# A two-layer graph network on one core: layer norm 2's sums on ScalarE, small factors on GpSimd, T1's four sums on VectorE, and new orders on every engine

## The chip, the cores and the metric

One core of one Trainium2 chip runs the whole program in one launch. The metric is the device time of one execution in microseconds (us), median of several runs. The core's engines are TensorE (PE in the profile, PEld for its weight loads), VectorE (DVE), ScalarE (ACT), GpSimd (POOL) and SyncE (SP), which here issues all the DMAs.

## The reference, cut to what matters

There are 128 graphs, each with 128 nodes and 512 features. For each graph (fp32):

```python
h  = relu(layernorm(x))                              # layer norm 0
A  = adj + I;  D = A.sum(-1) ** -0.5
x1 = x + (A * D[:,None] * D[None,:]) @ (h @ W + b)   # layer 0
xh = relu(layernorm(x1))                             # layer norm 1
H  = (adj != 0);  w = adj[0]                         # edge weights: the first row
P  = H @ diag(1/H.sum(0)) @ H.T;  dn = 1/(H @ w), 0 where H @ w is not positive
z  = relu(dn * (P @ (xh @ W1.T)) + b1)               # 1024 wide
hn = layernorm(z) * gamma + beta                     # layer norm 2
out = x1 + xh + dn * (P @ (hn @ W2.T)) + b2
```

## The kernel before, in words

The unit of work is a pair of graphs, `p` (64 pairs, `NP`); `g` is a graph (128, `NG`), `k` the number of a step of the steady loop. Every fp32 matrix is split into two fp16 parts, high and low, and every product is three matmuls (high by high, high by low, low by high). The high part is made by ScalarE, the low part by VectorE, so both stand in the chain of each product.

TensorE does for each graph `Y0` (h by W, 12 matmuls of 512 columns into the bank `ps_e`), `Z0` (A by that, 3, into the same bank `ps_e`), `T1` (xh by P, 12 short ones into `ps_t`), `U` (hn by W2, 24, into `ps_u`) and `Y2` (P by that, 3, into `ps_y2`). For each pair the product by W1 is one step of a Strassen-like scheme: seven products `M1` to `M7` of 6 matmuls each into `ps_x`, `ps_y`, `ps_z`, instead of eight. `P(p)` makes the matrix P and, in a 129th column, H @ w for both graphs in `ps_p`.

VectorE takes `Y0` out of `ps_e` (`yv`, then `yl`), and `x1(g)` takes `Z0` out of `ps_e` and adds x. `Y0` of the next graph waits for that `x1`, since both use `ps_e`. `z1` to `z7` take the seven products out of PSUM and add them into `zh`. `do_h` (ScalarE) is the relu on `zh`; `do_s2` and `do_aggr2` (VectorE) take mean and variance of 1024 values by batch-norm statistics; `do_u2`, `do_sc2` (GpSimd) and `do_nm2` (VectorE) turn them into scale and bias; `do_hn` (ScalarE) applies them; `do_hn_hi` (ScalarE) and `do_hn_lo` (VectorE) split the result, which DMAs transpose for `U`. After `U`, `do_uh` (ScalarE) and `do_ul` (VectorE) split it for `Y2`, and `do_out` (VectorE) makes the result.

The scheme of seven products needs four sums of quarters of T1 (`S1` to `S4`, 128x256 fp32), which GpSimd makes in SBUF once both `T1` are kept (`do_tf`); `do_thS` and `do_tlS` split them. GpSimd also makes `x1b`, `scr2` and `base2` (the part x1 + xh + b2 of the result, 128x512 fp32) and the small factors `rd0`, `cx`, `u1`, `sc1`, `dn1`, `dn2`, `qdn`.

The order on each engine is a list written out by hand. It has a beginning, a loop over pairs (`for k in range(STEADY_FROM, STEADY_TO)`) in which each engine works on several pairs at different stages, and an end. Engines meet by semaphores: `done(eng, s, n)` waits until `s` has counted to `n`, and `landed` waits for a DMA. In the names that the profile prints, buffer numbers are left out and aliases show as the tensor they lie in: `raw_w` is `zh`, `y`, `yh`, `yl`, `uh`, `ul`, `vq` or the result, `bet_wide` is `hn_hi` or `hn_lo`, `raw_t` is the transposed hn, `b_all` is `x1b` or `b1_all`, and `ps_y` is `ps_y` or `ps_y2`.

Of the kernel before, what the change touches and what calls it, by code (L numbers as in the profile page):

```python
# [5 lines left out]
def bass_adjacency_prenorm_two_layer_gnn_kernel(  # L6
# [52 lines left out]
    with ctx:  # L59
# [173 lines left out]
        def _(sp):  # L233
# [95 lines left out]
            do_ldX(10); do_tr0h(8); do_tr0h(9); do_trl(0); do_tr0l(8); do_trh(1); do_tr0l(9); do_ldA(10); do_trl(1)
            do_trA(6); do_ldX(11); do_ldX(12); do_trh(2); do_trl(2); do_tr0h(10); do_ldA(11); do_st(0); do_tr0l(10)  # L330
            do_tr0h(11); do_st(1); do_trh(3); do_tr0l(11); do_trl(3); do_ldX(13); do_trA(7); do_ldw(9); do_trh(4)
            do_ldA(12); do_trl(4); do_ldw(10); do_tr0h(12); do_st(2); do_tr0l(12); do_trh(5); do_st(3); do_ldX(14)
            do_tr0h(13); do_tr0l(13); do_trl(5); do_trA(8); do_ldX(15); do_trh(6); do_ldA(13); do_trl(6)
            do_tr0h(14); do_ldw(11); do_st(4); do_tr0l(14); do_trh(7); do_st(5); do_ldX(16); do_trl(7); do_tr0h(15)
            do_tr0l(15); do_trA(9); do_ldX(17); do_ldA(14); do_tr0h(16); do_trh(8); do_trl(8); do_ldw(12); do_st(6)
            do_tr0l(16); do_trh(9); do_st(7); do_trl(9); do_ldX(18); do_tr0h(17); do_tr0l(17); do_ldw(13)
            do_trA(10); do_ldX(19); do_ldA(15); do_trh(10); do_trl(10); do_tr0h(18); do_tr0l(18); do_st(8)
            do_trh(11); do_st(9); do_trl(11); do_ldX(20); do_tr0h(19); do_tr0l(19); do_ldw(14); do_trA(11)
# [1201 lines left out]
```

## Time and profile before

| | us |
|---|---|
| median of 3 runs | 1993.31 (1990.59 to 1993.95) |
| the profiled execution, its own time | 1991.01 |
| its span, first to last instruction | 1989.2 |
| TensorE busy | 1884.0 (95%) |
| VectorE busy | 1845.1 (93%) |
| ScalarE busy | 1292.1 (65%) |
| GpSimd busy | 1039.0 (52%) |

The span leaves 1.8 us of the execution's own time outside it. A busy share is a mean over the beginning, the loop and the end, which have different limits. The granted clock of TensorE has a mean of 0.99 of full speed over the span.

### The profile page before, as it was taken

The numbers are of one execution on the slowest core, as the hardware profiler recorded it, in microseconds if no ns is written. First come the engines' busy times: TensorE is split into PE (matmuls) and PEld (weight loads), VectorE is DVE, ScalarE is ACT, GpSimd is POOL, SyncE is SP. The second block draws the span as 40 slices with busy tenths as digits, with TensorE's granted clock in tenths as the row PEclk, the third lists the DMA queues.
The fourth block names the chain that finished last, engine by engine and source line by source line (L and its number), as shares of the span: only waits on it lengthen the run. The fifth ranks groups of instructions, "written<-read, shape, count | busy, mean of one in ns | idle before, by whom it ended". The sixth has DMA issues, their size and how long they took to land. (4 is left out here: it accounts for less than half of the span.)

```text
span 1989.2 us, 36929 instructions
## 1 busy us (share of the span) xinstructions
PE 1884.0 (95%) x9926; PEld 898.9 (45%) x9926; DVE 1845.1 (93%) x3751; ACT 1292.1 (65%) x2342; POOL 1039.0 (52%) x1234
## 2 busy tenths in 40 slices
PE   4688999999999999999999999999999999999998
PEld 2334444444444444444444444444444444444443
DVE  7999999999999999999999999999999999998864
ACT  5766666766766666676676676676667667667553
POOL 3656555455555555555546545555555554654541
PEclk9889999999999999999999999999999999999999
DMA  8235354544445445445444544544544444444333
GB/s 210 46 74 108 81 107 105 93 102 108 97 95 108 98 97 108 102 101 104 105 91 104 107 96 100 108 101 96 107 102 99 104 102 94 102 100 86 83 64 75
DMA packets 536734, 197.57 MB, mean 99 GB/s; under 512 B 484944, under 2 KB 501328, under 8 KB 536528
## 3 DMA queue, kind: packets, MB, share of 16 engines
q1 hardware_dynamic: 536528, 195.21, 46.9%
q8 instruction: 82, 1.34, 0.3%
q14 instruction: 124, 1.02, 0.2%
HBM read 48.31 MB, written 33.55 MB: 41 GB/s over the span
## 5 line engine op out<-in xcount | busy, mean ns | idle before, releaser
L381 PE MATMUL ps_u<-w2h,raw_t 128*128 128x512 f16 x2048 | 484.7, 379 | 6.7 <-DVE raw_w L1051 6.1
L1392 POOL TENSOR_TENSOR base<-b_all,xh 128x512 f32<-128x512 f32 x128 | 210.1, 1641 | 352.7 <-DVE raw_w L1060 344.4
L381 PEld LDWEIGHTS ps_u<-w2h,raw_t 128*128 128x128 f16 x2048 | 198.6, 98 | 252.4 <-issue 22.9
L381 PE MATMUL ps_u<-w2l,raw_t 128*128 128x512 f16 x1024 | 241.9, 379 | 0.0
L1046 DVE TENSOR_TENSOR bet_wide<-raw_w,bet_wide 128x1024 f16<-128x1024 f32 x128 | 211.3, 1650 | 8.4 <-ACT bet_wide L714 8.1
L681 ACT ACTIVATE tS<-ps_t 128x512 f32<-128x512 f32 x128 | 76.2, 595 | 205.2 <-PE ps_t L371 205.0
L638 ACT ACTIVATE raw_w<-v_all,qdn 128x512 f32<-128x512 f32 x128 | 85.8, 714 | 164.9 <-POOL qdn L1437 162.8
L1397 POOL TENSOR_TENSOR base<-base,raw_w 128x512 f32<-128x512 f32 x128 | 182.4, 1425 | 19.3 <-ACT raw_w L638 1.7
L1359 POOL TENSOR_TENSOR rd<-u,neg_half 128x4 f32<-128x4 f32 x64 | 70.0, 1094 | 201.8 <-DVE u L900 201.7
L381 PE MATMUL ps_e<-w0h,h0T_hi 128*128 128x512 f16 x512 | 134.6, 386 | 34.2 <-DVE x L939 34.0
L1386 POOL TENSOR_TENSOR b_all<-x,b_all 128x512 f32<-128x512 f32 x128 | 164.8, 1287 | 1.3
L1026 DVE BATCH_NORM_STATS2 raw<-raw_w 128x6 f32<-128x512 f32 x256 | 160.6, 671 | 2.5 <-ACT raw_w L700 2.5
L705 ACT ACTIVATE raw_w<-raw_w,nm,sc 128x1024 f32<-128x1024 f32 x128 | 156.7, 1232 | 7.1 <-DVE nm L1038 5.9
L392 PE MATMUL ps_x<-w1h,th 128*128 128x512 f16 x512 | 152.9, 380 | 5.2 <-issue 4.8
L381 PEld LDWEIGHTS ps_u<-w2l,raw_t 128*128 128x128 f16 x1024 | 100.2, 98 | 120.8
L392 PE MATMUL ps_x<-w1l,th 128*128 128x512 f16 x512 | 152.7, 380 | 0.0
L392 PE MATMUL ps_x<-w1h,tl 128*128 128x512 f16 x512 | 152.7, 380 | 0.0
L983 DVE SCALAR_TENSOR_TENSOR raw_w<-ps_x,dn,b_all 128x512 f32<-128x512 f32 x192 | 142.4, 742 | 3.9 <-PE ps_x L392 3.9
L700 ACT ACTIVATE raw_w<-raw_w 128x1024 f32<-128x1024 f32 x128 | 134.7, 1053 | 8.8 <-DVE raw_w L983 8.4
L714 ACT ACTIVATE bet_wide<-raw_w 128x1024 f16<-128x1024 f32 x128 | 134.0, 1047 | 6.5 <-DMA raw_t<-bet_wide 6.5
L381 PE MATMUL ps_e<-w0l,h0T_hi 128*128 128x512 f16 x512 | 134.0, 385 | 0.0
L381 PE MATMUL ps_e<-w0h,h0T_lo 128*128 128x512 f16 x512 | 132.3, 381 | 0.0
(151 smaller groups left out, 4517.5 us busy)
## 6 DMA issues: line engine op xcount, KB each, us to landing
x_t<-in_x_dram SPq DMA_DIRECT2D x128, 256.0 KB, 2.9
out_dram<-raw_w SPq DMA_DIRECT2D x128, 256.0 KB, 2.4
adj_t<-in_adj_dram SPq DMA_DIRECT2D x64, 128.0 KB, 2.1
raw_t<-bet_wide SPq DMA_TRANSPOSE x256, 3.2
w_col<-in_adj_dram SPq DMA_DIRECT2D x128, 0.5 KB, 2.2
raw_w<-in_W1T_dram SPq DMA_DIRECT2D x4, 512.0 KB, 4.8
h0T_hi<-h_hi SPq DMA_TRANSPOSE x128, 2.5
h0T_lo<-h_lo SPq DMA_TRANSPOSE x128, 2.4
```

Source lines behind the costliest of these rows:

```text
L381: mm = pe.matmul(ps, t[:, j * 128:(j + 1) * 128], w[:, j, :], start=(n == 0 and j == 0), stop=(n == 2 and j == blocks - 1))
L392: mm = pe.matmul(ps[:, :], t[:, t_at - 1, j * 128:(j + 1) * 128], w[:, w_at, j, :], start=(begins and n == 0 and j == 0), stop=(n == 2 and ...
L638: act.activation(vq[:, j, :], v_all[:, :], ACT.Copy, scale=qdn[:, p % 2, j:j + 1]).then_inc(s_vq, 1)
L700: act.activation(zh[:, g % 4, :], zh[:, g % 4, :], ACT.Relu).then_inc(s_h, 1)
L705: act.activation(zh[:, g % 4, :], zh[:, g % 4, :], ACT.Identity, bias=nm2[:, p % 2, j:j + 1], scale=sc2[:, p % 2, j:j + 1]).then_inc(s_hn, 1)
L714: act.activation(hn_hi[:, :], zh[:, g % 4, :], ACT.Copy).then_inc(s_hnh, 1)
L983: return dve.scalar_tensor_tensor(out=z, in0=bank[:, :], scalar=dn1[:, p % 2, j:j + 1], in1=z if row is None else row[:, cols], op0=ALU.mu ...
L1026: dve.bn_stats(raw2[:, g % 2, c, :], zh[:, g % 4, c * CH:(c + 1) * CH]).then_inc(s_rw2, 1)
L1046: dve.tensor_tensor(hn_lo[:, :], zh[:, g % 4, :], hn_hi[:, :], ALU.subtract).then_inc(s_hnl, 1)
L1386: pool.tensor_tensor(x1b[:, :], x1[:, g % 4, :], b2_all[:, :], ALU.add).then_inc(s_x1b, 1)
L1392: pool.tensor_tensor(base[:, g % 6, :], x1b[:, :], xh[:, g % 2, :], ALU.add).then_inc(s_scr2, 1)
L1397: pool.tensor_tensor(base[:, g % 6, :], base[:, g % 6, :], vq[:, g % 2, :], ALU.add).then_inc(s_base2, 1)
```

## The change

Five things change, and then all orders.

1. Layer norm 2. `do_h` also sums its output while it applies the relu (`hsum`). VectorE makes minus the mean of both graphs of the pair in one small operation (`do_nmu`). ScalarE squares `zh` with that as bias and sums it (`do_sq`, once for each graph, its product thrown away into `sq_scrap`), and GpSimd makes scale and bias. `do_s2`, `do_aggr2` and VectorE's `do_nm2` are gone.
2. `do_bias0`, `do_nm1` and `do_nm2` go to GpSimd; the first two are done for one graph at a time (128x1), and ScalarE waits for its own graph's.
3. The four sums `do_S1` to `do_S4` go from GpSimd to VectorE, with the same operation and size.
4. `do_dn` reads H @ w from PSUM (`ps_pp[:, :, N]`) and no longer from `dm` in SBUF, and the next `P` waits for it and no longer for `do_dm`.
5. The orders: the loop runs from pair 5 and no longer from pair 7, and to `NP - 16` and no longer `NP - 9`, and the order in the loop, in the beginning and at the end is another on every engine. SP's list loads `adj` of the first pairs ahead of its edge weights. No matmul and no DMA is added or taken away.

```diff
-    STEADY_FROM, STEADY_TO = 7, NP - 9
+    STEADY_FROM, STEADY_TO = 5, NP - 16
-            do_ldw(0); do_ldA(0); do_ldw(1); do_ldA(1); do_ldw(2); do_ldA(2); do_ldw(3); do_ldX(0); do_ldX(1)
+            do_ldA(0); do_ldw(0); do_ldA(1); do_ldw(1); do_ldA(2); do_ldw(2); do_ldX(0); do_ldX(1); do_ldA(3)
...
-                done(pe, s_dm, p)
+                done(pe, s_dn, p)
...
-                act.activation(zh[:, g % 4, :], zh[:, g % 4, :], ACT.Relu).then_inc(s_h, 1)
+                done(act, s_nmu, p - 1)
+                act.activation(zh[:, g % 4, :], zh[:, g % 4, :], ACT.Relu, accum_out=hsum[:, p % 2, j:j + 1]).then_inc(s_h, 1)
+
+            def do_sq(g):
+                p, j = g // 2, g % 2
+                act.wait_ge(s_nmu, p + 1)
+                done(act, s_u2, p - 1)
...
+                done(act, s_sq, g)
+                act.activation(sq_scrap, zh[:, g % 4, :], ACT.Square, bias=nmu[:, p % 2, j:j + 1],
+                               accum_out=ssq[:, p % 2, j:j + 1]).then_inc(s_sq, 1)
...
                 dve.wait_ge(s_ri, p + 1)
+                dve.wait_ge(s_p, p + 1)
...
-                dve.scalar_tensor_tensor(out=dn[:, p % 2, :], in0=dm[:, :], scalar=TINY, in1=ri[:, :],
+                dve.scalar_tensor_tensor(out=dn[:, p % 2, :], in0=ps_pp[:, :, N], scalar=TINY, in1=ri[:, :],
                                          op0=ALU.is_gt, op1=ALU.mult).then_inc(s_dn, 1)
 
+            def do_nmu(p):
+                dve.wait_ge(s_h, 2 * p + 2)
+                done(dve, s_sq, 2 * p - 2)
+                done(dve, s_ln2, p - 1)
+                dve.tensor_scalar(nmu[:, p % 2, :], hsum[:, p % 2, :], -1.0 / DH, None, ALU.mult).then_inc(s_nmu, 1)
...
             def do_u2(p):
-                pool.wait_ge(s_stat2, 2 * p + 2)
+                pool.wait_ge(s_sq, 2 * p + 2)
...
+            def do_nm1(g):
+                p, j = g // 2, g % 2
+                pool.wait_ge(s_pp1, p + 1)
+                done(pool, s_xh, g - 3)
+                pool.tensor_scalar(nm1[:, p % 2, j:j + 1], st1[:, p % 2, j, 0:1], sc1[:, p % 2, j:j + 1], -1.0,
+                                   ALU.mult, ALU.mult).then_inc(s_ln1, 1)
```

How the loop's orders move is seen at three places. On TensorE, in the loop before, this is the piece from `Z0` of the even graph (`ps_e`, line 432) over `M5` and `T1` to `Y0` of the odd graph (`ps_e`, line 381); twelve rows of `T1` stand in it:

```order
L432 MATMUL ps_e<-raw_w,A_HT 128x512
L433 MATMUL ps_e<-raw_w,A_HT 128x512
L434 MATMUL ps_e<-raw_w,A_HT 128x512
L392 MATMUL ps_z<-w1h,th 128x512 x2
L392 MATMUL ps_z<-w1l,th 128x512 x2
L392 MATMUL ps_z<-w1h,tl 128x512 x2
L369 MATMUL ps_t<-P_hi,xh_hi 128x128
L370 MATMUL ps_t<-P_lo,xh_hi 128x128
L371 MATMUL ps_t<-P_hi,xh_lo 128x128
```

In the loop of the change `Z0` (line 444 now) is followed by `Y2` of an older graph (`ps_y`), the twelve rows of `T1` and `M7` (`ps_x`), and then comes `Y0` (line 393):

```order
L444 MATMUL ps_e<-raw_w,A_HT 128x512
L445 MATMUL ps_e<-raw_w,A_HT 128x512
L446 MATMUL ps_e<-raw_w,A_HT 128x512
L444 MATMUL ps_y<-raw_w,P_hi 128x512
L445 MATMUL ps_y<-raw_w,P_hi 128x512
L446 MATMUL ps_y<-raw_w,P_lo 128x512
L381 MATMUL ps_t<-P_hi,xh_hi 128x128
L382 MATMUL ps_t<-P_lo,xh_hi 128x128
L383 MATMUL ps_t<-P_hi,xh_lo 128x128
```

So the three matmuls of a `Y2` more lie between the even graph's `Z0` and the odd graph's `Y0` (nine matmuls of 512 columns and a `T1`, six and a `T1` before).

On VectorE, around the same `x1` (`x<-ps_e,cx,x_t`, line 939), the loop before has, behind a `z2` (`ps_y`), a result (`base`), `hn_lo` of the odd graph (`bet_wide`) and `P_lo`:

```order
L983 SCALAR_TENSOR_TENSOR raw_w<-ps_y,dn,raw_w 128x512
L1060 SCALAR_TENSOR_TENSOR raw_w<-ps_y,dn,base 128x512
L1046 TENSOR_TENSOR bet_wide<-raw_w,bet_wide 128x1024
L1125 TENSOR_TENSOR P_lo<-ps_p,P_hi 128x256
L939 SCALAR_TENSOR_TENSOR x<-ps_e,cx,x_t 128x512
L1130 TENSOR_SCALAR dm<-ps_p 128x2
```

and in the change the same `x1` (line 1002 now) stands behind a result, `h0_lo` and `z6` (`ps_x`), ahead of the second result and `P_lo`:

```order
L1097 SCALAR_TENSOR_TENSOR raw_w<-ps_y,dn,base 128x512
L978 TENSOR_TENSOR h_lo<-h,h_hi 128x512
L1039 SCALAR_TENSOR_TENSOR raw_w<-ps_x,dn,b_all 128x512
L1002 SCALAR_TENSOR_TENSOR x<-ps_e,cx,x_t 128x512
L1097 SCALAR_TENSOR_TENSOR raw_w<-ps_y,dn,base 128x512
L1167 TENSOR_SCALAR dm<-ps_p 128x2
L1162 TENSOR_TENSOR P_lo<-ps_p,P_hi 128x256
```

`hn_lo` of the odd graph is gone from in front of this `x1`; it stands at the end of the step now, ahead of the four sums.

On GpSimd, the loop before has from the four sums (`tS`) to `rd0` the factors of layer norm 2 (`u<-st`, `sc`), and then those of layer norm 1 (`u<-st,eps_t`, `sc`):

```order
L1407 TENSOR_TENSOR tS<-tS 128x256
L1402 TENSOR_TENSOR tS<-tS 128x256
L1411 TENSOR_TENSOR tS<-tS 128x256
L1415 TENSOR_TENSOR tS<-tS 128x256
L1442 TENSOR_SCALAR u<-st 128x2
L1447 TENSOR_TENSOR sc<-u,neg_half 128x2
L1373 TENSOR_TENSOR u<-st,eps_t 128x2
L1378 TENSOR_TENSOR sc<-u,neg_half 128x2
L1359 TENSOR_TENSOR rd<-u,neg_half 128x4
```

and in the change `u1` and `sc1` of layer norm 1 come first, then `u2` (`u<-ssq`, which waits for both sums of squares), and behind it the two `nm1` (`nm<-st,sc`) for which ScalarE's `xh` waits:

```order
L1482 TENSOR_TENSOR u<-st,eps_t 128x2
L1487 TENSOR_TENSOR sc<-u,neg_half 128x2
L1533 TENSOR_SCALAR u<-ssq 128x2
L1553 TENSOR_SCALAR nm<-st,sc 128x1 x2
L1539 TENSOR_TENSOR sc<-u,neg_half 128x2
L1559 TENSOR_TENSOR nm<-nmu,sc 128x2
L1468 TENSOR_TENSOR rd<-u,neg_half 128x4
L1546 TENSOR_SCALAR bias<-st,rd 128x1 x2
```

The four sums are gone from GpSimd, and the two `nm1` of layer norm 1 are queued behind layer norm 2's `u2`. ScalarE's loop ends with the second `do_sq`, and the next step begins with `do_uh`, one `do_cntH` and the two `do_xh`.

## Rows read from the trace of the kernel before

**Rows 1.** The page: the span and each engine's busy time, share and instructions.

```profile
span 1989.2 us, 36929 instructions
PE 1884.0 (95%) x9926; PEld 898.9 (45%) x9926; DVE 1845.1 (93%) x3751; ACT 1292.1 (65%) x2342; POOL 1039.0 (52%) x1234
```

**Rows 2.** Busy time in four stretches: length, PE, PEld, DVE, ACT, POOL, granted clock, DMA share, GB/s.

```profile
0.00:50.00 50.00, 20.70 (x106) 11.58 (x107) 35.44 (x102) 26.28 (x81) 16.45 (x25) 0.93 0.81 210
50.00:300.00 250.00, 212.23 (x1075) 98.55 (x1074) 237.72 (x463) 162.96 (x298) 143.15 (x153) 0.94 0.40 83
300.00:1700.00 1400.00, 1376.26 (x7316) 659.56 (x7315) 1337.30 (x2752) 938.85 (x1709) 751.37 (x901) 1.00 0.49 102
1700.00:1989.00 289.00, 274.77 (x1433) 129.19 (x1431) 234.66 (x438) 164.06 (x259) 128.02 (x156) 1.00 0.41 83
```

**Rows 3.** TensorE's waits over the whole span: us in total, times, longest.

```profile
PE ps_e L381 <- DVE x L939: 34.0, 58, 3.3
```

**Rows 4.** TensorE's waits from 300 to 1700 us, the two largest.

```profile
PE ps_e L381 <- DVE x L939: 21.7, 48, 0.8
PE ps_u L381 <- DVE raw_w L1051: 1.5, 3, 0.7
```

**Rows 5.** Line 444, from 300 to 1700 us (two for a pair): least, median, greatest ns.

```profile
L444 PE MATMUL ps_p<-HB_hi,A_HT x94: 220/220/221, 317.2 to 1672.8; 128*128 128x129 f16 x94
```

**Rows 6.** TensorE in order of time in one step: start, length, idle before.

```profile
1008.06 1.89 PE L381 MATMUL ps_u<-w2h,raw_t 128*128 128x512 f16 x8 [0.71 <-DVE raw_w L1051]
...
1013.24 0.38 PE L432 MATMUL ps_y<-raw_w,P_hi 128*128 128x512 f16 x1
...
1020.97 0.22 PE L371 MATMUL ps_t<-P_hi,xh_lo 128*128 128x128 f16 x1
1021.97 1.02 PE L381 MATMUL ps_e<-w0h,h0T_hi 128*128 128x512 f16 x4 [0.78 <-DVE x L939]
```

**Rows 7.** VectorE in order of time at the same place.

```profile
1018.64 2.19 DVE L1046 TENSOR_TENSOR bet_wide<-raw_w,bet_wide 128x1024 f16<-128x1024 f32 x1
...
1021.09 0.73 DVE L939 SCALAR_TENSOR_TENSOR x<-ps_e,cx,x_t 128x512 f32<-128x512 f32 x1
```

**Rows 8.** GpSimd in order of time at the same place.

```profile
1018.48 1.26 POOL L1386 TENSOR_TENSOR b_all<-x,b_all 128x512 f32<-128x512 f32 x1
1019.88 2.08 POOL L1392 TENSOR_TENSOR base<-b_all,xh 128x512 f32<-128x512 f32 x1
```

**Rows 9.** Lines 1046, 1141 and 1442 over the span: least, median, greatest ns.

```profile
L1046 DVE TENSOR_TENSOR bet_wide<-raw_w,bet_wide x128: 1196/1226/2283, 121.9 to 1970.0; 128x1024 f16<-128x1024 f32 x128
...
L1141 DVE SCALAR_TENSOR_TENSOR dn<-dm,ri x64: 151/659/1258, 17.8 to 1903.6; 128x2 f32<-128x2 f32 x64
...
L1442 POOL TENSOR_SCALAR u<-st x64: 191/782/1078, 110.3 to 1960.4; 128x2 f32<-128x2 f32 x64
```

**Rows 10.** Groups by line: count, busy us, mean ns, idle before.

```profile
L1026 DVE BATCH_NORM_STATS2 raw<-raw_w 128x6 f32<-128x512 f32 x256 | 160.6, 671 | 2.5 <-ACT raw_w L700 2.5
L705 ACT ACTIVATE raw_w<-raw_w,nm,sc 128x1024 f32<-128x1024 f32 x128 | 156.7, 1232 | 7.1 <-DVE nm L1038 5.9
...
L700 ACT ACTIVATE raw_w<-raw_w 128x1024 f32<-128x1024 f32 x128 | 134.7, 1053 | 8.8 <-DVE raw_w L983 8.4 <-issue 0.2
...
L1407 POOL TENSOR_TENSOR tS<-tS 128x256 f32<-128x256 f32 x64 | 47.3, 739 | 31.7 <-ACT tS L681 31.7
...
L1077 DVE TENSOR_TENSOR A_H<-ahat,A_H 128x256 f16<-128x256 f32 x64 | 28.1, 439 | 0.4 <-ACT A_H L614 0.4
...
L1032 DVE BATCH_NORM_AGGREGATE st<-raw 128x2 f32<-128x12 f32 x128 | 25.3, 199 | 0.0
L629 ACT ACTIVATION_READ_ACCUMULATOR P_hi<-ps_p 128x1 f32 x128 | 25.1, 196 | 0.0
```

**Rows 11.** ScalarE in order of time, first and last of twelve instructions without a gap.

```profile
1008.92 1.51 ACT L666 ACTIVATE xh<-x,nm,sc 128x512 f32<-128x512 f32 x2
...
1015.34 1.05 ACT L714 ACTIVATE bet_wide<-raw_w 128x1024 f16<-128x1024 f32 x1
```

More of the change, by code:

```diff
@@ L329, in _ @@
[L329 to L338, printed above, removed]
@@ L734, in _ @@
-            square_sum_gamma(range(2, 3))
-            square_sum_gamma(range(3, 4))
             split_hi_w1(range(0, 1))
             split_hi_w1(range(1, 2))
+            split_hi_w1(range(2, 3))
+            split_hi_w1(range(3, 4))
+            split_hi_w1(range(4, 5))
+            square_sum_gamma(range(2, 3))
+            split_hi_w1(range(5, 6))
+            split_hi_w1(range(6, 7))
+            square_sum_gamma(range(3, 4))
             square_sum_gamma(range(4, 5))
             square_sum_gamma(range(5, 6))
-            split_hi_w1(range(2, 3))
@@ L901, in do_u0 @@
                                          op0=ALU.add, op1=ALU.mult).then_inc(s_u0, 1)
-            def do_bias0(p):
-                m = p % 2
-                dve.wait_ge(s_pp0, p + 1)
-                done(dve, s_h0, 2 * p - 2)
-                done(dve, s_h0h, 2 * p - 2)
-                dve.scalar_tensor_tensor(out=bias0[:, m, :], in0=st0[:, m, :, 0], scalar=-1.0, in1=rd0[:, m, :, 0],
-                                         op0=ALU.mult, op1=ALU.mult).then_inc(s_ln0, 1)
             def do_h0_lo(g):
@@ L949, in do_aggr1 @@
                 dve.wait_ge(s_rw1, g + 1)
-                done(dve, s_ln1, p - 1)
+                done(dve, s_ln1, g - 3)
                 dve.bn_aggr(st1[:, p % 2, j, :], raw1[:, j, :]).then_inc(s_stat1, 1)
-            def do_nm1(p):
-                m = p % 2
-                dve.wait_ge(s_pp1, p + 1)
-                done(dve, s_xh, 2 * p - 2)
-                dve.scalar_tensor_tensor(out=nm1[:, m, :], in0=st1[:, m, :, 0], scalar=-1.0, in1=sc1[:, m, :],
-                                         op0=ALU.mult, op1=ALU.mult).then_inc(s_ln1, 1)
             def do_xh_lo(p):
@@ L1133, in do_ri @@
                 dve.wait_ge(s_dm, p + 1)
+                done(dve, s_dn, p)
                 dve.reciprocal(ri[:, :], dm[:, :]).then_inc(s_ri, 1)
@@ new lines, in do_S1, with do_S3, do_S2 @@
+            def do_S1(p):
+                dve.wait_ge(s_tf, 2 * p + 2)
+                done(dve, s_tls, p)
+                dve.tensor_tensor(tS[:, S1, :], tS[:, A21, :], tS[:, A22, :], ALU.add).then_inc(s_s1, 1)
+            def do_S3(p):
+                dve.wait_ge(s_tf, 2 * p + 2)
+                done(dve, s_tls, p)
+                dve.tensor_tensor(tS[:, S3, :], tS[:, A11, :], tS[:, A21, :], ALU.subtract).then_inc(s_s3, 1)
+            def do_S2(p):
+                dve.wait_ge(s_s1, p + 1)
+                dve.tensor_tensor(tS[:, S2, :], tS[:, S1, :], tS[:, A11, :], ALU.subtract).then_inc(s_s2, 1)
@@ L1168, in _ @@
             split_lo_w1(range(0, 1))
             split_lo_w1(range(1, 2))
-            do_aggr1(1)
+            do_w_hi(4)
             split_lo_w1(range(2, 3))
-            do_nm1(0)
+            do_w_lo(4)
+            split_lo_w1(range(3, 4))
             keep_beta_row()
+            split_lo_w1(range(4, 5))
+            split_lo_w1(range(5, 6))
+            do_yv(2)
+            split_lo_w1(range(6, 7))
             weight_magnitude(2)
-            split_lo_w1(range(3, 4))
+            do_bn0(4); do_yl(2); do_aggr0(4)
```

886 lines of the change are left out of this document (501 added, 385 removed).

## The prediction

> **What bounds the kernel now.** I read the page first, then the stretches, TensorE's waits, and last one step in order of time. TensorE is busy for 95% of the span and VectorE for 93% [rows 1]. The stretches split this: in the first 50 us TensorE works for 20.7, from 50 to 300 for 212.2 of 250, from 300 to 1700 for 1376.3 of 1400, and behind that for 274.8 of 289 [rows 2]. VectorE is busy for 237.7 of the 250 us of the second stretch and for 1337.3 of 1400 in the third: it is nearly full wherever TensorE waits. The granted clock is 0.93 and 0.94 of the 2.4 GHz in the first two stretches, and 1.00 behind them.
>
> A step of the loop (one pair) takes (1672.8 - 317.2) / 46 = 29.47 us, since 94 rows of line 444 are 47 pairs [rows 5]. TensorE's own work in it: `U` starts 24 matmuls in 1013.24 - 1008.06 = 5.18 us, 0.216 each [rows 6]. A pair has 126 such matmuls (27.2 us) and 28 of 128 or 129 columns at a quarter of that (1.5), so 28.7. A step loses 0.75 us.
>
> Nearly all of it is one wait: `Y0` on `x1`, 48 times in that stretch, 21.7 us, and little else (1.5 us for `ul`) [rows 4]. Over the span it is 34.0 us in 58 times [rows 3]. The row understates it: a matmul counts 0.38 us as busy [rows 6], but the next may start 0.216 after it, so each wait costs 0.16 more. In the loop that is 21.7 + 48 x 0.16 = 29.4 us.
>
> Why is `x1` late? In the step shown, `T1` starts its last matmul at 1020.97 and `Y0` begins only at 1021.97 [rows 6]. VectorE started `x1` at 1021.09, behind an `hn_lo` of 2.19 us that began at 1018.64 [rows 7]. The same operation takes 1.23 us by its median [rows 9]. Here GpSimd had begun an `x1b` 0.16 us before it, which ran to 1019.74 [rows 8]: `hn_lo` did not move until GpSimd had finished, and then took its 1.1 us. That is a second cost of a full VectorE: an operation with two inputs in SBUF stands still while GpSimd works. `dn` shows it too, 0.66 us at the median against 0.15 at least, for two elements [rows 9]; and the other way round GpSimd's `u2` takes 0.78 at the median and 0.19 at least.
>
> **The change, part by part**, for one pair.
>
> Layer norm 2 off VectorE: four statistics at 0.671 and two aggregates at 0.199 go, 3.1 us, and `bias0`, `nm1`, `nm2` about the 0.2 of the aggregate each, 0.6 [rows 10]. `nmu` adds a small operation, at most 0.2. The four sums come: the nearest rows are 0.439 for 256 elements of the same operation [rows 10] and a quarter of `hn_lo`'s 1.226 for 1024, 0.31 [rows 9], so 1.2 to 1.8; I take 1.4. `dn` now has one input in PSUM, as `x1` has, which took its 0.73 us from 1021.09 on while GpSimd's next operation ran [rows 7, 8]; it gives back 0.5. `hn_lo` of the odd graph moves from in front of `x1` to the end of the step, where GpSimd has few large operations left: up to 1.0. VectorE's sum is -3.7 + 0.2 + 1.4 - 0.5 - 1.0, some 3.6 us off 1337.3 / 47.5 = 28.2 us a step: its load falls to about 25.
>
> ScalarE gets two squares like the relu's 1.053 and four reads of an accumulator at 0.196: 2.9 us a pair [rows 10]. It is busy for 938.9 of 1400 us, 19.8 a step [rows 2], and goes to 22.7 of 28.7. Throughput hides it; where its cover is thin is below. GpSimd loses four sums at 0.739, 3.0 us, and gains five small operations of 0.19 to 0.78 each (1.0 to 3.9; I take 1.5); with 751.4 of 1400 us it bounds nothing by its load.
>
> The Trainium skill (GPSIMD Engine Reference, Key points) says that GpSimd shares its SBUF interfaces with VectorE and contends with VectorE instructions that have two SBUF inputs. The trace agrees (2.19 against 1.23 above). The rule speaks against the four sums on VectorE, since each is such an instruction. Were each held by one GpSimd operation of 1.26 us [rows 8], VectorE would have 30 us a step, 1.3 above TensorE's own 28.7, and the sum below would be 1955 + 47 x 1.3 = 2016; by the order, which puts them where GpSimd has mostly small ones, it stays at 1955.
>
> The orders: in the loop `x1` of the even graph has, behind `Z0`, nine matmuls and a `T1` of room, 9 x 0.216 + 0.65 = 2.6 us, against 1.9 before, and in front of it only `z6` of what depends on TensorE in that time. `z6` must wait for `M6`, which ends with `Z0`'s start; `z6` and `x1` at 0.74 each are done 1.6 us ahead of `Y0`. So the 29.4 us should go: **-29**.
>
> The beginning: TensorE stands for 37.8 us between 50 and 300 us with VectorE 95% full, and part of it is the ten `x1` waits outside the loop (12.3 us). Some six pairs pass there, each 2 to 3.6 us lighter on VectorE: 12 to 22 us. The weights' splits stay. I let half of the middle reach TensorE, -9, and -3 for waits at the end, where layer norm 2's latency hardly changes (two statistics, aggregate and `nm2` on VectorE go, a square and its read come). **-12**, bounds 0 and -25.
>
> New waits: **+5**. They come from one chain whose cover is thin. ScalarE's last operation of a step is the second square; `u2` on GpSimd waits for it, and both `nm1` are queued behind `u2`; `xh` waits for them at ScalarE's start of the next step, and behind `xh` are queued `thS`, `xh_hi`, `hn`, `h0_hi` twice, `yh`, `hn_hi`, `hn`, `uh`; then VectorE's `ul`, `z5`, `out`; for this last the odd graph's `Y2` waits. The second square ends about when TensorE's step ends (`M4` ends 6.5 us before that, and `z4`, `h`, `thA`, two squares and the small ones of ScalarE add to 6.5). From there TensorE has 60 matmuls up to that `Y2`, 12.95 us. ScalarE's run of twelve instructions took 6.4 us from `xh` to `hn_hi` [rows 11]; without `h0` twice and `P_hi`, with `thS`, another `hn_hi` and two `hn` at 1.23 less the overlap [rows 10], it is 9.5 to the end of `uh`. VectorE's three add 2.1. GpSimd's three small operations add 0.6 (each 0.19) to 2.3 (each 0.78). Total 12.2 to 13.9: cover of 0.75 us, or a wait of 0.95. I take a tenth of a us a step (47 x 0.1), because at that time GpSimd's neighbours on VectorE are mostly single-input ones.
>
> **Sum**: 1991.0 - 29 - 12 + 5 = 1955 for the profiled execution's own time, which is 2.3 below the median of the three runs and inside their spread; the forecast of the median is **1955.5**.
>
> **Rivals.**
> - *The relief is eaten in part.* Either the sums stand still behind GpSimd (two held by 1.0 us a step), so that `x1` of the odd graph and `tlA` ahead of `M1` come late, or the chain above costs 0.3 to 0.5 a step. For it: `hn_lo` reaches 2.28 [rows 9]. Against: `M1` waits at the end of the step, when GpSimd's six large operations have run. 47 steps at 0.4 give 1955 - 5 + 19, some **1970 to 1985**. 2 in 10.
> - *It doesn't do what it says.* VectorE was full, but another chain through `ps_e` is just as long, and the wait stays at `Y0` in another place. Against it: the 1.6 us above. **1987 to 1996**. 0.6 in 10.
> - *The other side: `nm1` behind `u2`.* The chain above with its upper bound (0.95) and one more hold, a `hn_lo` of the even graph at 2.19 for 1.23 in half the steps: 1.4 us a step. It decides from 0.75 us a step on, which is what a step loses today. 1991 - 12 + 47 x (1.4 - 0.75) is **2010**. 1.1 in 10. For it: `u2` has a median of 0.78 today, so it is usually held. Against: today it runs beside `tlA`, in the change beside the small ones.
> - *More than forecast*: the beginning gives 25 or more, **under 1940**. 0.3 in 10.
> - The forecast itself, 1940 to 1968: 6 in 10.
>
> **How the numbers follow.** A measurement of this kernel can tell about 0.2% (4 us) from no change. Faster holds the forecast, the first rival and the last: 0.6 + 0.2 + 0.03 = 0.83. Same takes most of the second rival, 0.06, slower the third, 0.11. The range from 1938 to 1986 leaves out the second and third rivals and most of the last. The forecast's own range is 1940 to 1968.
>
> **What the profile after would show.** Right: the group of `Y0`'s waits on `x1` falls from 34 us to under 10; a step in the loop is 28.7 to 29.0 us; VectorE's busy time is near 1650 and the odd graph's `hn_lo` no longer at 2.2; `dn` is near 0.16; ScalarE's busy time is near 1480, GpSimd's near 940. Wrong: TensorE waits at `Y2` for `out`, or ScalarE's `xh` waits long on `nm1` (the chain); the sums' mean is over 0.6 us (held); or 50 to 300 us shows TensorE idle as much as before, and then the -12 was not there.

## The result, and the profile after

The changed kernel takes **1948.35 us** (median of 4 runs, 1944.31 to 1949.87) against 1993.63 for the kernel before beside it. The ratio is 0.9769, with a 95% interval from 0.9748 to 0.9791. The forecast was 1955.5. The profiled execution took 1944.31 us, its span is 1942.4.

The page of the kernel after, its busy times (as [rows 1]), and the four stretches (as [rows 2]; columns are the stretch, then busy us and number of instructions of PE, PEld, DVE, ACT and POOL, the granted clock, DMA share and GB/s):

```profile
PE 1877.9 (97%) x9926; PEld 893.7 (46%) x9926; DVE 1665.5 (86%) x3495; ACT 1465.3 (75%) x2726; POOL 995.2 (51%) x1298
```

```profile
0.00:50.00 50.00, 26.56 (x116) 12.59 (x117) 34.70 (x99) 25.86 (x71) 22.23 (x33) 0.93 0.80 216
50.00:300.00 250.00, 225.66 (x1185) 105.77 (x1183) 228.41 (x473) 193.90 (x373) 136.78 (x172) 0.96 0.44 90
300.00:1700.00 1400.00, 1393.72 (x7424) 666.12 (x7422) 1225.46 (x2610) 1089.08 (x2034) 741.43 (x968) 1.00 0.51 103
```

TensorE now works for 26.6 of the first 50 us (20.7 before) and for 225.7 of the next 250 (212.2 before). VectorE is no longer full: 1225 of 1400 us in the loop, for 1337 before. TensorE's waits, first over the whole span (as [rows 3]), then from 300 to 1700 us (as [rows 4]); columns are us in total, times, longest:

```profile
PE ps_p L456 <- DVE HB_lo L1155: 13.7, 1, 13.7
PE ps_e L444 <- DVE raw_w L993: 10.6, 9, 4.6
PE ps_e L393 <- DVE x L1002: 6.2, 6, 2.4
```

```profile
PE ps_y L444 <- DVE raw_w L1097: 5.0, 14, 0.5
PE ps_e L444 <- DVE raw_w L993: 0.4, 1, 0.4
```

The 34.0 us in which `Y0` waited for `x1` are down to 6.2, and none of it lies in the loop. What is left there is `Y2` (`ps_y`) waiting for `out` (line 1097). A step took 29.47 us before and takes 29.03 now, both by the starts of `P` from 300 to 1700 us. Two of VectorE's groups, over the whole span (shortest, median and longest in ns), show that the holds of [rows 9] are gone too; the odd graph's `hn_lo` takes 1.26 us by its mean, 2.08 before:

```profile
L1083 DVE TENSOR_TENSOR bet_wide<-raw_w,bet_wide x128: 1210/1224/2245, 111.5 to 1923.3; 128x1024 f16<-128x1024 f32 x128
```

```profile
L1180 DVE SCALAR_TENSOR_TENSOR dn<-ps_p,ri x64: 125/136/160, 16.0 to 1860.2; 128x2 f32<-128x2 f32 x64
```

So that stretches of kernels of different speed can be compared, I cut each execution by TensorE's own work. Each matmul's columns count 0.2156 us per 512 (the starts in [rows 6]). The 22 fp32 matmuls of the beginning count twice that: the twelve shown here start 0.43 us apart.

```profile
41.56 5.39 PE L439 MATMUL ps_y<-raw_w,bet_wide 128*128 128x512 f32 x12
```

This adds to 1845.2 us in every kernel that computes all of this. The time beyond that is what TensorE loses, by waits or by a lower clock:

| lost, us, in the part of TensorE's own work | first 250 | next 1350 | up to the last 50 | last 50 |
|---|---|---|---|---|
| before | 89.3 | 36.6 | 6.9 | 11.1 |
| after | 67.6 | 16.4 | 2.0 | 11.2 |
| gain | 21.7 | 20.2 | 4.9 | -0.1 |

Up to 5 us of the first gain is clock: the granted clock from 50 to 300 us was 0.94 before and is 0.96 now, and 0.02 of 250 us is 5.

### The profile page after: what moved, and what is told of

Same layout as the page of the kernel before. It is cut to its first block, busy times and chain, and to the rows that moved or that the text cites. A ratio compares the mean times of both kernels' runs of the same rounds, so it can differ in the third digit from the quotient of the medians.

```text
span 1942.4 us, 37250 instructions
## 1 busy us (share of the span) xinstructions
PE 1877.9 (97%) x9926; PEld 893.7 (46%) x9926; DVE 1665.5 (86%) x3495; ACT 1465.3 (75%) x2726; POOL 995.2 (51%) x1298
## 4 chain that ended last, share of the span: by engine, by line
PE 87%; issue 5%; DVE 4%; POOL 2%; DMA 1%; ACT 1%; SPq 1%; DVEq 0%; POOLq 0%; ACTq 0%
PE ps_u L393 33%; PE ps_e L393 16%; PE ps_x L404 14%; PE ps_z L404 8%; PE ps_y L404 4%; PE ps_y L444 2%; PE ps_t L382 1%; PE ps_t L383 1%; PE ps_t L381 1%; PE ps_y L445 1%; PE ps_e L444 1%; PE ps_y L446 1%; PE ps_e L446 1%; PE ps_e L445 1%; DVE raw_w L1097 1%
## 5 line engine op out<-in xcount | busy, mean ns | idle before, releaser
L1501 POOL TENSOR_TENSOR base<-b_all,xh 128x512 f32<-128x512 f32 x128 | 196.3, 1533 | 408.3 <-DVE raw_w L1097 399.6
L667 ACT ACTIVATE raw_w<-v_all,qdn 128x512 f32<-128x512 f32 x128 | 92.0, 721 | 245.2 <-POOL qdn L1528 233.1
L1083 DVE TENSOR_TENSOR bet_wide<-raw_w,bet_wide 128x1024 f16<-128x1024 f32 x128 | 158.8, 1241 | 20.9 <-ACT bet_wide L755 20.9
L1506 POOL TENSOR_TENSOR base<-base,raw_w 128x512 f32<-128x512 f32 x128 | 163.3, 1276 | 13.5 <-ACT raw_w L667 13.3
L740 ACT ACTIVATE raw_w<-raw_w,nmu 128x1024 f32<-128x1024 f32 x128 | 145.4, 1136 | 0.8 <-DVE nmu L1187 0.2
L993 DVE SCALAR_TENSOR_TENSOR raw_w<-raw_w 128x512 f16<-128x512 f32 x128 | 88.5, 691 | 64.4 <-ACT raw_w L688 64.4
L1482 POOL TENSOR_TENSOR u<-st,eps_t 128x2 f32<-128x2 f32 x64 | 18.3, 286 | 223.5 <-DVE st L1014 223.5
```

The source lines that it names most:

```text
L667: act.activation(vq[:, j, :], v_all[:, :], ACT.Copy, scale=qdn[:, p % 2, j:j + 1]).then_inc(s_vq, 1)
L740: act.activation(sq_scrap, zh[:, g % 4, :], ACT.Square, bias=nmu[:, p % 2, j:j + 1], accum_out=ssq[:, p % 2, j:j + 1]).then_inc(s_sq, 1)
L1083: dve.tensor_tensor(hn_lo[:, :], zh[:, g % 4, :], hn_hi[:, :], ALU.subtract).then_inc(s_hnl, 1)
L1501: pool.tensor_tensor(base[:, g % 6, :], x1b[:, :], xh[:, g % 2, :], ALU.add).then_inc(s_scr2, 1)
L1506: pool.tensor_tensor(base[:, g % 6, :], base[:, g % 6, :], vq[:, g % 2, :], ALU.add).then_inc(s_base2, 1)
```

## Experiments

The kernels below all do the whole computation. Their orders are written out without a loop, so their line numbers differ from those above; I name the operations. "Over after" is the difference to 1948.35 us. Runs of the kernel before beside them had medians of 1993.07 to 1994.3. Waits, busy times and steps are those of one profiled execution of each kernel.

### Layer norm 2's statistics back on VectorE

```diff
 VectorE, in the place of do_nmu(p):
-do_nmu(p)
+do_s2(2p); do_aggr2(2p); do_s2(2p+1); do_aggr2(2p+1)
 ScalarE:
-do_sq(2p) ... do_sq(2p+1)
```

> The changed kernel with layer norm 2's statistics back on VectorE (four statistics, two aggregates where nmu stood; no squares on ScalarE), all orders kept. Theory (VectorE's load was what held TensorE): VectorE gets about 2.9 us a pair back and stands near 28 us a step, over 90% busy; waits for x1, raw_w or tlA return, a step is 29.4 to 30.0 us and the time 1968 to 1995. Rival (the new orders alone did it, with x1 better placed): the time stays within 4 us of 1948, at most 1952, though VectorE's busy time rises by 150 us or more.

Measured 2112.25 us, ratio 1.06 (1.0586 to 1.0615): 164 over after, and more than either theory allowed. VectorE is busy for only 1832.3 us, 87% of the span. ScalarE's and TensorE's largest new waits, each from 300 to 1700 us:

```profile
ACT xh L814 <- POOL nm L2034: 135.6, 44, 3.4
```

```profile
PE ps_y L504 <- DVE raw_w L1323: 54.0, 44, 1.6
PE ps_x L464 <- issue: 46.3, 44, 1.4
```

The block of 3.0 us stands in front of the odd graph's `x1`, `tlA` and `st1`. So `u1`, `sc1` and `nm1` are late, `xh` waits 3.1 us for them (0.04 after), and the delay goes on through `uh`, `ul` and `out` to `Y2`; `M1` (`ps_x`) starts 1.1 us late behind `tlA`. The same block was moved behind `aggr1`, where it delays none of those:

```diff
 VectorE: ... x1(odd) S2 tlA S4 st1 Hu aggr1(odd)
+do_s2(2p); do_aggr2(2p); do_s2(2p+1); do_aggr2(2p+1)
 GpSimd:
-do_u2(p); do_nm1(g); do_nm1(g+1)
+do_nm1(g); do_nm1(g+1); do_u2(p)
```

> The changed kernel with layer norm 2's statistics back on VectorE, but behind aggr1 of the odd graph (58 pairs) and not in front of its x1, and with nm1 ahead of u2 on GpSimd. In the first such kernel (2112 us) the block of 3.0 us stood in front of x1, tlA, st1 and so of u1, sc1, nm1 and xh. Theory placement: x1, tlA and nm1 are on time again, the block now delays tlS, u0 and hn only, and the time is 1965 to 2000, at least 100 us less than with the same load in front of x1. Theory load (VectorE with about 28 us a step has no place for it anywhere): 2060 or more.

Measured 2063.26 us, ratio 1.0352 (1.0335 to 1.0368), 49 less than in the first place and 115 over after. By its numbers this is the answer foreseen for the load, but the waits show another chain in its place. ScalarE and TensorE, from 300 to 1700 us:

```profile
ACT h_hi L793 <- POOL bias L2027: 124.5, 45, 3.1
```

```profile
PE ps_u L453 <- DVE raw_w L1314: 58.2, 45, 1.6
PE ps_y L504 <- DVE raw_w L1323: 25.0, 46, 0.6
```

Now `u0` stands behind the block, and `rd0`, `bias0` and `h0_hi` are late with it; `uh` and `ul` are queued behind `h0_hi`. A step is 30.95 us (31.77 in the first place), while VectorE is busy for 88% of the span. So two things hold: the place is worth 0.8 us a step, and in both places the 2.9 us cost 1.9 to 2.7 a step although VectorE stands idle for over 3 us of it. In neither place is the gap that it would need free of a chain; other places weren't tried. (The second kernel also has `nm1` ahead of `u2`, which alone makes no difference that can be told, see below.)

### The same relief in the old orders

```diff
 before.py, VectorE:
-do_s2(2p) ... do_aggr2(2p) do_s2(2p+1) ... do_aggr2(2p+1)
+do_nmu(p)          (in the place of the second aggregate)
 ScalarE, behind thA(p+1):
+do_sq(2p); do_sq(2p+1)
```

> The kernel before with its own orders, in which layer norm 2's sums alone are taken over by ScalarE (sum of h in the relu, a square of each graph behind the second thA or h of its pair); nmu in the place of the second aggregate, everything else where it was. Theory 1 (VectorE's load, 28.2 us a step before, is what made x1 late): it loses 2.9 us a pair, Y0's 34 us of waits on x1 fall to under 10 and the time is 1945 to 1965, also with the old orders. Theory 2 (after what the kernel with the statistics back on VectorE showed: what counts is how long the operations are that stand in front of x1, T1's differences and nm1, not the load): also here four statistics in front of x1 and tlA are gone, so it gains as well, but the odd graph's held hn_lo still stands in front of x1, so 5 to 15 us of that wait stay and the time is 1960 to 1980. Rival (the new orders were needed for any gain): ScalarE's squares stand in front of thS and hn in the old order, TensorE waits there instead, 1985 or more.

Measured 2046.72 us, ratio 1.0271 (1.0256 to 1.0286): the rival. VectorE is 105 us less busy than before (1739.9), and the kernel is 53 us slower. VectorE's own first wait from 300 to 1700 us, and TensorE's:

```profile
DVE cm L1412 <- ACT HB_lo L776: 92.6, 47, 2.7
```

```profile
PE ps_e L458 <- DVE x L1271: 35.7, 46, 0.8
PE ps_u L458 <- DVE raw_w L1376: 16.6, 46, 1.1
```

ScalarE's squares stand in front of the counts (`cntH`) that VectorE's `cm` needs. VectorE waits 2.0 us a step for them (6.8 us in all before, 92.6 here), and what is queued behind `cm` comes late. Most of the relief of 2.9 us is spent as a wait. I tried no other place for the squares in the old orders.

### `x1` ahead in the old orders

```diff
 before.py, VectorE, 52 pairs:
-do_hn_lo(g+1); do_P_lo(p); do_x1(g)
+do_x1(g); do_hn_lo(g+1); do_P_lo(p)
```

> The kernel before with x1 of the even graph moved ahead of the odd graph's hn_lo and of P_lo on VectorE (52 pairs), nothing else. Theory placement (x1 was late since the held hn_lo of 2.19 us stood in front of it): Y0's wait on x1 falls from 34 us to under 8, and 15 to 25 us are gained, 1968 to 1980. Theory load (VectorE is full, whatever is moved ahead makes something else late): hn_lo and P_lo come 0.7 us later, TensorE waits there or at M or Y2 instead, and the time stays within 5 us of 1993.

Measured 2049.85 us, ratio 1.0286 (1.0271 to 1.0302), 56 slower. `Y0`'s wait on `x1` did fall, from 34.0 to 10.4 us, as the theory of placement said. The time went up by a way that neither theory had. One step of it, on VectorE, GpSimd, SP (DMA issues), and VectorE again; start, duration, engine and line:

```profile
1016.27 0.75 DVE L1245 SCALAR_TENSOR_TENSOR x<-ps_e,cx,x_t 128x512 f32<-128x512 f32 x1 [0.56 <-PE ps_e L510]
1016.94 2.32 DVE L1352 TENSOR_TENSOR bet_wide<-raw_w,bet_wide 128x1024 f16<-128x1024 f32 x1
...
1023.85 0.69 DVE L1194 BATCH_NORM_STATS2 raw<-x_t 128x6 f32<-128x512 f32 x1 [1.37 <-DMA x_t<-in_x_dram]
...
1025.27 0.66 DVE L1236 SCALAR_TENSOR_TENSOR raw_w<-raw_w 128x512 f16<-128x512 f32 x1
```

```profile
1016.92 1.26 POOL L1990 TENSOR_TENSOR base<-b_all,xh 128x512 f32<-128x512 f32 x1
```

```profile
1019.29 1.24 SPq L296 DMA_TRANSPOSE raw_t<-bet_wide  x1
1020.63 0.52 SPq L250 DMA_DIRECT2D x_t<-in_x_dram  x1
```

`x1`, moved ahead, waits for `Z0` (0.56 us). The `hn_lo` behind it is still held by GpSimd (2.32 us) and now ends at 1019.26. Its transpose is next on SP's queue, which works in order, and behind the transpose stands the load of `x_t`. That lands late, VectorE's statistics wait 1.37 us for it, and `yl` behind them is what TensorE waits for, in all 46 steps from 300 to 1700 us:

```profile
DVE raw L1194 <- DMA x_t<-in_x_dram: 62.4, 46, 3.2
```

```profile
PE ps_e L508 <- DVE raw_w L1236: 64.5, 46, 3.3
```

Before, the first of these waits was 1.3 us in 2 times, and the second 0.2. No kernel tests the link through SP's queue by itself; it is read from the trace.

### `dn` from SBUF again

```diff
-in0=ps_pp[:, :, N]      (do_dn)
+in0=dm[:, :]
```

> The changed kernel with dn reading its first operand from SBUF again, as before the change; nothing else. Theory (the operation with two SBUF inputs stands still while GpSimd works): dn is held again in part of the pairs, its median goes from 0.136 us to 0.3 to 0.7, VectorE's busy time rises by 10 to 30 us, and since VectorE has room the time rises by 0 to 4 us. Rival (dn's hold in the kernel before was its place, not its operand): the median stays under 0.2 us.

Measured 1990.24 us, ratio 0.9986 (0.9977 to 0.9995): 42 over after, for an operand of two elements. `dn` takes 1.075 us by its mean (0.137 after, 0.605 before); 59 of its 64 executions began beside a `base` of GpSimd and were held. One step on VectorE and on GpSimd shows why:

```profile
1009.59 1.18 DVE L1430 SCALAR_TENSOR_TENSOR dn<-dm,ri 128x2 f32<-128x2 f32 x1
```

```profile
1009.50 1.26 POOL L1983 TENSOR_TENSOR base<-base,raw_w 128x512 f32<-128x512 f32 x1
```

GpSimd began 0.09 us earlier; `dn` ends 0.01 us after it. TensorE's waits, whole span:

```profile
PE ps_p L516 <- DVE dn L1430: 40.1, 56, 1.0
```

In this kernel TensorE's next `P` still waited for `dn`, as in the change, where it must since `dn` reads that bank. The next one takes this wait away too, as before the change:

```diff
-done(pe, s_dn, p)       (do_P)
+done(pe, s_dm, p)
```

> The changed kernel with dn reading dm in SBUF, and TensorE's next degree matmuls waiting for dm alone, as both were before the change (in the first such kernel TensorE still waited for dn itself, 40.1 us in 56 times, and dn took 1.075 us by its mean). Theory: dn is held by GpSimd for about 1 us as there, but nothing waits for it at once, so VectorE's busy time rises by 60 us and the time by only 0 to 5 us, to 1948 to 1954. Rival (1 us of VectorE in front of st1, aggr1 and the next outputs matters by itself): 1960 or more, with the wait for out (Y2) or for x1 longer than in the changed kernel.

Measured 1973.06 us, ratio 0.9899 (0.9882 to 0.9915), 25 over after: the rival. `dn` still takes 1.077 us. Nothing waits for `dn` itself, but `yl` and with it `Z0` come later (16.4 us from 300 to 1700, 0.4 after). So 25 us are the price of the held `dn`, 0.94 us a pair of VectorE's time at that place with what it moves, and 17 more that of the wait. One thing that it moves is `w_hi`, which now begins beside a `base` too and takes 0.91 us by its mean, for 0.25 after. By itself that costs little: with `bias0` back on VectorE (below) `w_hi` takes 0.87 us, and that kernel has the shortest step of all. The other way round, the same edit alone in the kernel before:

> The kernel before with dn alone changed: its first operand in PSUM, and TensorE's next degree matmuls waiting for dn in place of dm (two dn of the beginning moved up so that this can be). Theory: dn goes from 0.605 to 0.14 us and VectorE gets 0.47 us a pair back, close behind the odd hn_lo and x1; at most the 0.47 reach TensorE: 1970 to 1990. Rival (in the old orders dn stood where its hold cost nothing, since GpSimd's next operation is waited for anyway): 1990 to 1996. Other side (what starts earlier meets a GpSimd operation, as with out first): over 1998.

Measured 1988.68 us, ratio 0.998 (0.9971 to 0.9988), 4.4 us faster. `dn` takes 0.150 us, but `Y0`'s wait for `x1` only falls from 34.0 to 32.2. VectorE's largest wait from 300 to 1700 us takes up the rest:

```profile
DVE raw_w L1229 <- PE ps_e L457: 31.1, 48, 0.7
```

It is `yv` that now stands 0.65 us a step for `Y0`. VectorE was 93% busy before, and yet what was taken off at this place came back as idle time.

### T1's sums back on GpSimd

```diff
 VectorE:
-do_S1(p) do_S2(p) do_S3(p) do_S4(p)
 GpSimd, in front of do_u1(p+1):
+do_S3(p); do_S1(p); do_S2(p); do_S4(p)
```

> The changed kernel with T1's four sums back on GpSimd (ahead of u1 of the next pair, as they stood before the change), the rest kept. Theory (VectorE's load decides, GpSimd has room): VectorE loses 1.65 us a pair, GpSimd gains 3.0; the large operations of GpSimd again stand beside VectorE's two-input ones, so hn_lo and P_lo are held more often; time 1945 to 1955. Rival (moving the sums was needed, since GpSimd's small operations of the chain u1, sc1, u2, nm1 now stand behind them): nm1 comes late, ScalarE waits for it, Y2 waits for out longer, and the time is over 1958.

Measured 1945.93 us, ratio 0.9765 (0.9748 to 0.9781): no difference to after. GpSimd's busy time goes from 995 to 1203 us, VectorE's from 1666 to 1619. In the new orders it makes no difference to the time who makes the sums.

### `bias0` back on VectorE, and `nm1` ahead of `u2`

```diff
 VectorE, in front of xh_lo(p-2):
+do_bias0(p)             (both graphs, 128x2)
 GpSimd:
-do_bias0(2p); do_bias0(2p+1)
```

> The changed kernel with bias0 (both graphs in one operation, 128x2) back on VectorE, ahead of xh_lo two pairs earlier; the rest kept. Theory: ScalarE's h0_hi no longer waits the 0.40 us a pair for GpSimd's two bias0, which were held by tlS and xh_lo, so the chain xh to uh is up to 0.4 us shorter and the wait of Y2 for out (0.25 us a step) shrinks: time 1938 to 1948. Rival (the chain's length up to uh is set elsewhere, or VectorE pays as much): within 2 us of 1948; above 1952 if VectorE's one operation is itself held by GpSimd.

Measured 1943.35 us, ratio 0.9752 (0.9738 to 0.9765), 5 under after. The intervals overlap by a little, but the step says it more sharply: 28.84 us for 29.03. `Y2` starts late 6 times and for 0.9 us in all between 300 and 1700, for 48 times and 11.9 us after, counted from start to start. TensorE's waits there are all small:

```profile
PE ps_e L504 <- DVE raw_w L1251: 0.3, 1, 0.3
PE ps_u L453 <- DVE raw_w L1346: 0.2, 1, 0.2
PE ps_y L504 <- DVE raw_w L1355: 0.2, 1, 0.2
```

The other link of that chain:

```diff
-do_u2(p); do_nm1(g); do_nm1(g+1)
+do_nm1(g); do_nm1(g+1); do_u2(p)
```

> The changed kernel with both nm1 ahead of u2 on GpSimd (56 pairs), the rest kept. Theory (the chain u2, nm1, xh is what the odd graph's Y2 waits for, 0.25 us a step): xh starts 0.29 us earlier (u2 from start to start), and with it the chain to uh, ul and out; the wait at Y2 shrinks and the time is 1936 to 1947. Rival (ScalarE's h0_hi in the chain waits for GpSimd's bias0, so what xh gains is lost there): within 2 us of 1948. Other side (tlS and xh_lo start earlier than bias0 or later, so that the holds fall elsewhere): over 1955.

Measured 1944.55 us, ratio 0.976 (0.9745 to 0.9776). This isn't told apart from after (1948.35), and the step is the same, 29.05 us. `Y2` is late 26 times instead of 48, for 9.9 us instead of 11.9, and ScalarE's wait for `bias0` goes from 22.1 to 24.0 us. ScalarE's idle time in front of `xh`, gaps under 0.15 us included, was only 4.9 us to begin with and falls to 1.8; most of that comes back at `bias0`, and `Z0` waits 3 us more for `yl`.

### `out` ahead of `z5`

```diff
 VectorE, 56 pairs:
-do_z5(p); do_out(g)
+do_out(g); do_z5(p)
```

> The changed kernel with VectorE's out ahead of the adjacent z5 (56 places), the rest kept. Theory (the wait of 0.25 us a step that is left in the loop is that of the odd graph's Y2 for out, which stands behind a z5 of 0.65 us): out ends 0.66 us earlier, the wait is gone, a step goes from 29.03 to 28.8 us, the time to 1935 to 1942. Rival (z5 frees a bank of PSUM for which TensorE waits next): within 3 us of 1948.

Measured 2016.04 us, ratio 1.0121 (1.0103 to 1.014), 68 over after and 1.2% slower than before. The wait of `Y2` is gone, as the theory said, and a step takes 30.41 us. TensorE has two new waits instead, from 300 to 1700 us, a product into `ps_x` for its `z` and `P` for `dn`:

```profile
PE ps_x L464 <- DVE raw_w L1289: 31.6, 46, 1.1
PE ps_p L516 <- DVE dn L1430: 29.4, 45, 0.7
```

In the kernel after, VectorE and then GpSimd:

```profile
1012.83 0.74 DVE L1097 SCALAR_TENSOR_TENSOR raw_w<-ps_y,dn,base 128x512 f32<-128x512 f32 x1
1013.49 0.68 DVE L978 TENSOR_TENSOR h_lo<-h,h_hi 128x512 f16<-128x512 f32 x1
```

```profile
1013.74 1.57 POOL L1501 TENSOR_TENSOR base<-b_all,xh 128x512 f32<-128x512 f32 x1 [6.46 <-DVE raw_w L1097]
```

And with `out` first, VectorE and then GpSimd:

```profile
1021.73 0.74 DVE L1347 SCALAR_TENSOR_TENSOR raw_w<-ps_y,dn,base 128x512 f32<-128x512 f32 x1
1022.39 0.74 DVE L1289 SCALAR_TENSOR_TENSOR raw_w<-ps_z,dn,b_all 128x512 f32<-128x512 f32 x1
1023.05 1.41 DVE L1228 TENSOR_TENSOR h_lo<-h,h_hi 128x512 f16<-128x512 f32 x1
```

```profile
1022.64 1.27 POOL L1978 TENSOR_TENSOR base<-b_all,xh 128x512 f32<-128x512 f32 x1 [5.79 <-DVE raw_w L1347]
```

`out` frees the buffer that GpSimd's `scr2` (`base<-b_all,xh`) waits for. In the kernel after `h0_lo` starts 0.25 us before `scr2`, and it is `scr2` that stands still (1.57 us for 1.27). With `out` first `scr2` wins by 0.41 us, and `h0_lo` waits it out: 1.41 us, and 1.370 by its mean over 128, 0.706 after. It is so in nearly every step: from 300 to 1700 us `h0_lo` begins while `scr2` runs 91 times with `out` first and never in the kernel after, where `scr2` begins while `h0_lo` runs 96 times. VectorE loses 1.3 us a step there, and 0.7 more at `w_hi`, which now starts behind a `base` too (mean 0.908 us, 0.246 after). To tell this from the rival, `out` stayed first and only `scr2` was kept back:

```diff
 do_scr2(g), even g from 8 on:
+pool.wait_ge(s_z5, (g - 2) // 2 + 1)
```

> The kernel with out ahead of z5 (2016 us; there h0_lo took 1.37 us by its mean for 0.71, held by GpSimd's base, which out had released 0.66 us earlier), and beside it GpSimd's base of the even graph waits for z5 too, so that it starts no earlier than in the changed kernel. Theory (hold): h0_lo is back at 0.70 to 0.75 us, out is early for Y2, and the time is 1935 to 1946. Rival (it was z5, 0.66 us later, whose bank of PSUM M7 waited for): the waits ps_x for raw_w stay at over 25 us and the time over 1985.

Measured **1942.33 us**, ratio 0.9747 (0.9734 to 0.976): the lowest of all, and 74 us less than without the wait. `h0_lo` is back at 0.719 us and again always ahead of `scr2`, a step is 28.95, TensorE's wait into `ps_x` is down from 31.6 to 2.5 us and the one for `dn` is gone. So it was the hold and not `z5`. A wait more on GpSimd, idle for half of the span, gives back the whole loss. Whether it beats the kernel after (by 6 us) the intervals, which overlap by a little, don't quite settle; its step is 0.08 us shorter.

## Why the prediction was right, point by point

**-29, `Y0` waits for `x1`.** Right, mechanism and size. All 48 waits in the loop are gone, 29.4 us, and the odd graph's `hn_lo`, now at the end of the step, is held no more. Only the margin was too wide: I had `x1` done 1.6 us ahead of `Y0`; in the step shown it ends at 1015.49 and `Y0` starts at 1016.33, 0.84 us. The held `hn_lo` of [rows 7] was the cause: `x1` moved ahead of it in the old orders took 24 of the 34 us of this wait away. That this alone cost 56 us elsewhere I hadn't seen; the -29 holds for the new orders as a whole.

**-12, beginning and end.** The size was off: 21.7 in the beginning and 4.9 at the end, 26.6, just outside the bound of 25. The beginning has two sources. In the first 50 us TensorE works 5.9 us more; the kernel with the statistics back on VectorE has that too (26.43), and the relief in the old orders hasn't (20.95), so it comes from the new order of the first instructions, which I hadn't priced. And with the statistics back the first part loses 85.3 us for 67.6 after, 17.7 more, where I had let only half of 12 to 22 reach TensorE. But that isn't the relief's by itself: in the old orders the same relief made the first part lose 102.3 us for 89.3. Here too relief and orders only work together, and how they share the gain stays open.

**+5, the chain to `Y2`.** The end of the chain was right, from `h0_hi` over `uh`, `ul` and `z5` to `out` and `Y2`; the size was 11.9 us, 0.25 a step and not 0.1. Its head was not. I had it start at the second square and go through `u2` and `nm1` to `xh`. But `xh` hardly waits for `nm1`, and `u2` starts 0.31 us (median) after the square has ended, right behind `sc1`. What makes `Y2` late is a link that I had missed: ScalarE's `h0_hi` stands in that chain and waits for GpSimd's `bias0` in every step, 0.46 us. ScalarE's waits, from 300 to 1700 us, and GpSimd in order of time:

```profile
ACT h_hi L674 <- POOL bias L1546: 22.1, 48, 0.9
ACT xh L695 <- POOL nm L1553: 1.8, 7, 0.3
```

```profile
1004.94 2.20 POOL L1546 TENSOR_SCALAR bias<-st,rd 128x1 f32<-128x1 f32 x2
```

Two operations on one column take 2.20 us there, since VectorE's `tlS` and `xh_lo` (1.22 us each, from 1004.49 and 1005.63) stand in their way. `bias0` back on VectorE took `Y2`'s wait away; `nm1` ahead of `u2`, the link that I had named, did little. `Y2` waiting for `out` was also one of the signs that I had named for being wrong, and it is there; the sum had room for it. I had taken five small operations at 1.5 us in all; `bias0` alone is 0.949 by its mean, twice a pair.

**The sum.** With the measured sizes it is 1991.0 - 29.4 - 26.6 + 11.9 = 1946.9; the profiled execution took 1944.3. About that difference is `U`'s wait for `ul`, 3.4 us from start to start in the loop before, which is gone and which I had at nothing. The forecast's 1955 was 11 too high, since the beginning was missed by more (14.6) than the chain (6.9). That the two errors have opposite signs was luck. So was part of the forecast of the median: I put it 0.5 above the profiled execution, while the medians stand 2.3 (before) and 4.0 (after) above theirs. VectorE's busy time (1665.5 for "near 1650"), ScalarE's (1465 for 1480), `dn` (0.136 for 0.16) and the step (29.03 for 28.7 to 29.0) came out as foreseen or close to it. GpSimd's was not: 995 for 940. The held `bias0` is more than that: 128 times 0.949 less 0.264, 88 us.

**`dn`, priced at 0.5 us of VectorE's time.** Right for the old orders, where it is worth 4.4 us. In the new ones it stands beside GpSimd's `base` and is worth 25 to 42: without it the change would have given 3 to 21 us instead of 45 (1993.6 less 1990.2 or 1973.1). I had costed the edit by what it saved, not by what the new place would have made of it.

**The sums on VectorE.** 0.42 us each (0.427 at most in 256), 1.4 to 1.7 a pair, and never held. The Trainium skill's rule (GPSIMD Engine Reference, Key points: GpSimd shares its SBUF interfaces with VectorE and contends with VectorE instructions that have two SBUF inputs) speaks against them, and the 2016 us that it would have made of them didn't come. But the rule as such is borne out everywhere else, by `dn` and by `h0_lo` above. That it didn't bite is the order's doing: 74 of the 256 sums meet an operation of GpSimd, each a small one of 128x2 or less, and none meets one of 512 columns. The move itself is worth nothing that the runs can tell (1945.9 with it undone).

**The idea behind it, "VectorE is full", holds only in part.** Less load in the old orders made the kernel 53 us slower (layer norm 2) or 4 us faster (`dn`); the load back in the new orders cost 115 to 164 us for 187 us of work (64 x (4 x 0.671 + 2 x 0.199 - 0.16)). In the places that were tried, neither the relief nor the one move in order that I named as the cure gives anything by itself. What was shown is that they are needed together: without the relief the new orders are slower than the old ones, without `dn`'s operand they keep 3 to 21 of 45 us, and the relief needs an order in which ScalarE's squares delay nothing. Which single moves of the new orders carry the 20 us in the loop stays open; they weren't taken apart further.

## What to carry to other kernels

Where in-order queues are tied this tightly, an average load says little: price a moved operation by what starts earlier or later because of it, on the engine that it releases and in the queue behind it, DMA queue included. Look for pairs of a large GpSimd operation and a VectorE one with two SBUF inputs that start within some tenths of a microsecond of each other; whoever starts first wins, so an edit that frees GpSimd earlier can cost 68 us, and one wait on the idle engine gives it back. Small factors are cheap in busy time and dear in a chain: look at what stands beside them before they go to GpSimd.
